# Rounded three-pass downs for seven more units, VectorE making both halves of w1 for the first four experts, in a recurrent layer with a mixture of experts

## The reference, cut to what matters

```python
# x: 32 sequences, 32 steps, 128 features. xw = x @ Wx + b
# scan: h_t = tanh(xw_t + h_(t-1) @ Wh)                      -> 1024 tokens of 128
xn = xf * rsqrt(mean(xf * xf) + EPS) * norm_scale
logits = xn @ wg + bg;  vals, idx = top_k(logits, 4);  gates = softmax(vals)   # spread over 16 experts
h = einsum('th,ehd->etd', xn, w1) + b1                       # 16 experts, 128 -> 256
a = minimum(h[..., ::2], 7.0); b = clip(h[..., 1::2], -7.0, 7.0)
s = a * sigmoid(1.702 * a) * (b + 1.0)
y = einsum('eti,eih->eth', s, w2) + b2                       # 128 -> 128
out = x + xf + einsum('eth,te->th', y, gate_full)
```

## Time and profile before

| | |
|---|---|
| median of 3 runs | 105.08 us (104.44 to 105.55) |
| profiled execution, its time | 105.43 us |
| profiled execution, its span | 103.2 us |
| TensorE busy (matmul) | 97.5 us, 94% |
| VectorE, ScalarE, GpSimd busy | 70.9, 68.8 and 69.2 us |
| one relu, one sigmoid-gelu, one act_high of 512 columns on ScalarE | 0.66, 0.66 and 0.62 us |
| granted TensorE clock | 1.00 |

### The profile page before, as it was taken

How to read it: one execution, slowest core, us unless ns; L and a number is a source line. 1 busy time by engine, 2 the same in 40 slices (tenths; PEclk the granted TensorE clock), 3 DMA queues, 4 the chain that set the end, 5 groups by cost and what they waited for, 6 DMA issues and landing times.

```text
span 103.2 us, 1831 instructions
## 1 busy us (share of the span) xinstructions
PE 97.5 (94%) x587; PEld 82.7 (80%) x588; DVE 70.9 (69%) x181; ACT 68.8 (67%) x162; POOL 69.2 (67%) x82
## 2 busy tenths in 40 slices
PE   7989997999999999999999999999999999999970
PEld 2657556799999799998999788888888888889950
DVE  0300569878859975898669987867886978878530
ACT  3224799799877893669857777556678688697000
POOL 6000287999394998089773999999659459859300
PEclk9999999999999999999999999999999999999999
DMA  2997970005980007960099301996010000000012
GB/s 71 202 295 245 393 291 12 6 10 136 332 341 6 6 6 179 386 248 3 16 267 389 154 0 17 259 352 241 6 51 3 0 0 0 0 0 0 6 51 51
DMA packets 5001, 12.99 MB, mean 126 GB/s; under 512 B 752, under 2 KB 1792, under 8 KB 4992
## 3 DMA queue, kind: packets, MB, share of 16 engines
q1 hardware_dynamic: 4672, 12.66, 36.7%
q10 hardware_dynamic: 320, 0.21, 0.7%
HBM read 12.28 MB, written 0.59 MB: 125 GB/s over the span
## 4 chain that ended last, share of the span: by engine, by line
PE 71%; DVE 13%; DMA 5%; ACT 4%; issue 2%; POOL 1%; SPq 1%; DVEq 0%; POOLq 0%
PE psA L910 19%; PE psB L910 17%; PE psY L954 6%; DMA wx_x_sb<-in_wx_x 5%; PE psR L954 5%; PE psM L945 3%; PE psY L945 3%; DVE lin L788 2%; PE psY L855 2%; DVE act L811 2%; PE psM L966 2%; PE psY L966 2%; PE psM L954 2%; PE psR L855 2%; PE psA L887 1%
## 5 line engine op out<-in xcount | busy, mean ns | idle before, releaser
L788 DVE TENSOR_SCALAR lin<-psB,one_b1b 128x256 f32<-128x256 f32 (+1 forms) x48 | 25.9, 568 | 11.9 <-PE psB L910 11.9
L589 ACT ACTIVATE psA<-psA,lim_b1a 128x256 f32<-128x256 f32 (+1 forms) x48 | 23.8, 511 | 14.1 <-PE psA L910 13.9
L461 POOL TENSOR_TENSOR actg<-act,gate_cols 128x512 f32<-128x512 f32 x25 | 31.8, 1281 | 1.7 <-DMA gate_cols<-gate_rows 1.7
L601 ACT ACTIVATE psA<-psA,limit_col 128x512 f32<-128x512 f32 x32 | 21.1, 658 | 0.8
L910 PE MATMUL psA<-xn_hi,w_hi 128*128 128x256 f32 (+1 forms) x48 | 18.8, 392 | 0.4 <-DVE act L811 0.3
L811 DVE SCALAR_TENSOR_TENSOR act<-lin,psA 128x512 f32<-128x512 f32 x26 | 17.9, 687 | 1.5 <-DVE lin L788 0.9
L910 PE MATMUL psB<-xn_hi,w_hi 128*128 128x256 f32 (+1 forms) x48 | 15.8, 329 | 0.0
L910 PE MATMUL psB<-xn_lo,w_hi 128*128 128x256 f32 (+1 forms) x48 | 15.3, 319 | 0.0
L910 PE MATMUL psB<-xn_hi,w_lo 128*128 128x256 f32 (+1 forms) x48 | 15.3, 318 | 0.0
L910 PE MATMUL psA<-xn_hi,w_lo 128*128 128x256 f32 (+1 forms) x48 | 15.2, 318 | 0.0
L910 PE MATMUL psA<-xn_lo,w_hi 128*128 128x256 f32 (+1 forms) x48 | 15.2, 319 | 0.0
(11 more groups left out here) (113 smaller groups left out, 182.9 us busy)
## 6 DMA issues: line engine op xcount, KB each, us to landing
gate_cols<-gate_rows SPq DMA_DIRECT2D x16, 512.0 KB, 5.4
w_sb<-in_w SPq DMA_DIRECT2D x4, 512.0 KB, 8.4
w_sb<-in_w SPq DMA_DIRECT2D x4, 256.0 KB, 9.6
out<-yT SPq DMA_DIRECT2D x3, 128.0 KB, 1.7
wx_x_sb<-in_wx_x SPq DMA_DIRECT2D x1, 320.0 KB, 5.5
wx_x_sb<-in_wx_x SPq DMA_DIRECT2D x2, 128.0 KB, 2.6
small_h<-in_small ACTq DMA_DIRECT2D x1, 105.0 KB, 2.7
gate_rows<-gT SPq DMA_DIRECT2D x4, 16.0 KB, 1.4
```

Source lines behind the costliest of these rows:

```text
L461: nc.gpsimd.tensor_tensor(by_pair(actg[:, u % SUM_DEPTH, w]), by_pair(act[:, u % ACT_DEPTH, w]), gate_block(u, w), ALU.mult).then_inc(actg ...
L589: last = nc.scalar.activation(psA[u % 2][:, o], psA[u % 2][:, o], ACT.Relu, scale=-1.0, bias=lim_b1a[:, e0 + k:e0 + k + 1])
L601: nc.scalar.activation(psA[u % 2][:, 0:w], psA[u % 2][:, 0:w], ACT.Gelu_apprx_sigmoid, scale=-1.0, bias=limit_col[:, :]).then_inc(swish_do ...
L788: last = nc.vector.tensor_scalar(lin[:, v % 2, o], psB[v % 2][:, o], one_b1b[:, e0 + k:e0 + k + 1], LIMIT + 1.0, ALU.add, ALU.min)
```

## The change

SPLIT grows from 8 units to 15: 12, 13 and 15 (two experts each) and 16 to 27 without a gap. Unit 12 also joins DVE_PRODUCT, so VectorE multiplies it by its gates. All of w2 is now split, in four parts of four experts in place of three runs of 2, 3 and 3. ScalarE makes the high parts at the ends of slots 6, 8, 12 and 14. GpSimd makes the low parts in its slots 9 (two of them), 13 and 16.

VectorE makes both halves of w1 for experts 0 to 3 at the start (w1_halves), where ScalarE made the high halves, and GpSimd and VectorE shared the low halves of experts 0 to 5. VectorE also makes the high half of gS (gates_halves), which was ScalarE's. At the start normalise(1) stands behind route_logits(0). On GpSimd power_rstd of pair 1 moves one slot ahead. On PE one x times Wx product leaves the gap after step 1, which waited for the last part of x, and one goes to the gap after step 7. The result goes to xn in place of yT.

```diff
     GROUP0 = list(range(CHUNKS[0])) + list(range(CHUNKS[0], NT + 1, 2))
-    W1_SHARED = 3
+    W1_DVE = 2
     XW_AT = [0, 3, 0, 1, 2, 1, 2, 3]
-    XW_GAP = {1: 5, 2: 6, 3: 7, 4: 3, 6: 4}
+    XW_GAP = {2: 5, 3: 6, 4: 3, 6: 4, 7: 7}
     NQ = NT // 2
...
     FIRST = UNIT0[NC - 1]
-    SPLIT = [u for u in range(FIRST + 2, NU - 4) if u % 4]
-    SPLIT_RUNS = [[u for u in SPLIT if u // 4 == k] for k in sorted({u // 4 for u in SPLIT})]
-    W2_HIGH, W2_LOW = [13, 14, 17], [16, 17, 18]
+    SPLIT = [FIRST - 4, FIRST - 3, FIRST - 1] + list(range(FIRST, NU - 4))
+    W2_ORDER = [2, 3, 0, 1]
+    W2_HIGH, W2_LOW = [6, 8, 12, 14], [9, 9, 13, 16]
+    EW = E // len(W2_ORDER)
     SPLIT_DEPTH = 3
-    DVE_PRODUCT = list(range(FIRST + 4, NU, 2))
+    DVE_PRODUCT = [FIRST - 4] + list(range(FIRST + 4, NU, 2))
...
     RSTD = [None] + [v + 1 for v in STATS[1:]]
+    POWER = [None, STATS[1] - 1] + STATS[2:]
     GATES = [0] + [v + 2 for v in STATS[1:]]
...
-        def w2_run(i):
-
-            run = SPLIT_RUNS[i]
-            k = SPLIT.index(run[0])
-            return slice(k, k + len(run)), slice(run[0] - FIRST, run[-1] + 1 - FIRST)
+        def w2_part(i):
+
+            return slice(W2_ORDER[i] * EW, (W2_ORDER[i] + 1) * EW)
...
-                pool.wait_ge(w1_hi_ready, 2 * p + a + 1)
+                pool.wait_ge(w1_hi_ready, 2 * (p - W1_DVE) + a + 1)
                 pe_ = slice(2 * p, 2 * p + 2)
...
-                to, es = w2_run(i)
+                es = w2_part(i)
                 pool.wait_ge(w2_hi_ready, i + 1)
-                nc.gpsimd.tensor_tensor(w2_lo[:, to, :], w2_sb[:, es, :], w2_hi[:, to, :].bitcast(F32),
+                nc.gpsimd.tensor_tensor(w2_lo[:, es, :], w2_sb[:, es, :], w2_hi[:, es, :].bitcast(F32),
                                         ALU.subtract).then_inc(w2_lo_ready, 1)
...
             power_rstd(1)
-            for p in range(W1_SHARED):
-                w1_low(p, 1)
+            for a in range(2):
+                w1_low(W1_DVE, a)
             power_expo(0)
             place_expo(0)
-            for p in range(W1_SHARED, NP):
+            for p in range(W1_DVE + 1, NP):
                 for a in range(2):
...
                     xn_low(pair_group(q))
-                for q in at(STATS, v):
+                for q in at(POWER, v):
                     power_rstd(pair_group(q))
+                for i in at(W2_LOW, v):
+                    w2_low(i)
                 for q in at(RSTD, v):
...
                     place_expo(q)
-                for i in at(W2_LOW, v):
-                    w2_low(i)
                 if v >= POOL_LAG and v - POOL_LAG not in DVE_PRODUCT:
...
-            def gates_low(q):
-
-                dve.wait_ge(gS_high, q + 1)
+            def gates_halves(q):
+
+                dve.wait_ge(gT_ready, q + 1)
                 low, qc = slice(LOW_AT, LOW_AT + E), slice(q * PW, (q + 1) * PW)
+                mark(nc.vector.tensor_copy(gS[:, qc], psX[0:GR, 0:PW]))
+                settled()
                 nc.vector.tensor_tensor(gS[low, qc], psX[low, 0:PW], gS[low, qc].bitcast(F32),
...
-            def w1_low(p):
+            def w1_halves(p):
+                dve.wait_ge(w1_loaded[2 * p // EG], 16)
                 pe_ = slice(2 * p, 2 * p + 2)
-                dve.wait_ge(w1_hi_ready, 2 * p + 1)
-                nc.vector.tensor_tensor(w1_lo[:, pe_, 0, :], w1_sb[:, pe_, 0, :], w1_hi[:, pe_, 0, :].bitcast(F32),
+                mark(nc.vector.tensor_copy(w1_hi[:, pe_, :, :], w1_sb[:, pe_, :, :]))
+                settled()
+                nc.vector.tensor_tensor(w1_lo[:, pe_, :, :], w1_sb[:, pe_, :, :], w1_hi[:, pe_, :, :].bitcast(F32),
                                         ALU.subtract).then_inc(w1_ready, 1)
...
             b2_parts()
+            w1_halves(0)
             stats(0)
-            w1_low(0)
+            w1_halves(1)
             normalise(0)
...
             copy_raw(pair_tiles(0), psB[0]).then_inc(raw_read, 1)
-            normalise(1)
             dve.wait_ge(consts_ready, 1)
             dve.wait_ge(bg_loaded, 16)
+            dve.wait_ge(raw_read, 1)
             route_logits(0)
+            normalise(1)
             route_top(0)
...
             route_hot(0)
-            w1_low(1)
-            w1_low(2)
             close_gates(0)
...
                         to = psX[:, 0:w]
+                        dve.wait_ge(gS_ready, NQ if v > LAST_T else NQ - 1)
                     else:
...
                     pe.wait_ge(gS_ready, q)
+                if q == NQ - 1:
+                    pe.wait_ge(actg_dve, 1)
                 for k, j in enumerate(pair_tiles(q)):
...
                     i = SPLIT.index(u)
-                    pe.wait_ge(w2_lo_ready, [u in run for run in SPLIT_RUNS].index(True) + 1)
+                    pe.wait_ge(w2_lo_ready, W2_ORDER.index((e0 + r - 1) // EW) + 1)
                     passes = ((w2_hi, act_hi), (w2_lo, act_hi), (w2_hi, act_lo))
...
                             pe.wait_ge(act_hi_ready, i + 1)
-                        for o, y in y_parts(c):
-                            last = nc.tensor.matmul(y, w[:, i, :], x_part[:, i % SPLIT_DEPTH, o], start=False, stop=False)
+                        for k in range(r):
+                            for o, y in y_parts(c):
+                                a = part(c, k) if r > 1 else o
+                                last = nc.tensor.matmul(y, w[:, e0 + k, :], x_part[:, i % SPLIT_DEPTH, a], start=False,
+                                                        stop=(m == 2 and e0 + k == E - 1))
                     last.then_inc(y_mm, 1)
...
                     x_wx(XW_GAP[t], 1, start=False)
-                elif t == TL + 1:
+                if t == TL + 1:
                     pe.wait_ge(consts_ready, 1)
...
```

More of the change, by code:

```diff
@@ L153, in adaln_rnn_moe_kernel @@
         act_lo = sb("act_lo", [P, SPLIT_DEPTH, W], F32R)
-        w2_hi = sb("w2_hi", [P, len(SPLIT), H], F32R)
-        w2_lo = sb("w2_lo", [P, len(SPLIT), H], F32R)
-        yT = sb("yT", [P, NT * P])
+        w2_hi = sb("w2_hi", [P, E, H], F32R)
+        w2_lo = sb("w2_lo", [P, E, H], F32R)
+        yT = xn
         psA = [pb("psA0"), pb("psA1")]
@@ L198, in adaln_rnn_moe_kernel @@
         gT_ready = sem("gT_ready")
-        gS_high = sem("gS_high")
         gS_ready = sem("gS_ready")
@@ L312, in w1_low_count @@
         def w1_low_count(p, a):
-            return p + 1 if p < W1_SHARED else 2 * p - W1_SHARED + a + 1
+            return p + 1 if p < W1_DVE else 2 * (p - W1_DVE) + a + 1
         def steps_at(u, slot):
@@ L544, in copy_gates @@
                 nc.scalar.activation(gT[:, qc], psX[0:E, 0:PW], ACT.Copy).then_inc(gT_ready, 1)
-                nc.scalar.activation(gS[:, qc], psX[0:GR, 0:PW], ACT.Copy).then_inc(gS_high, 1)
             def act_high(u):
@@ L556, in w2_high @@
             def w2_high(i):
-                to, es = w2_run(i)
+                es = w2_part(i)
                 for g in range(NG):
                     acte.wait_ge(w2_loaded[g], 16)
-                nc.scalar.activation(w2_hi[:, to, :], w2_sb[:, es, :], ACT.Copy).then_inc(w2_hi_ready, 1)
+                nc.scalar.activation(w2_hi[:, es, :], w2_sb[:, es, :], ACT.Copy).then_inc(w2_hi_ready, 1)
             acte.wait_ge(small_loaded, 16)
@@ L570, in _ @@
                 elif t >= W1_AT:
-                    w1_high(t - W1_AT)
+                    w1_high(2 * W1_DVE + t - W1_AT)
             acte.wait_ge(consts_ready, 1)
-            for k in range(HEAD - 1 - W1_AT, 2 * NP):
+            for k in range(2 * W1_DVE + HEAD - 1 - W1_AT, 2 * NP):
                 w1_high(k)
@@ L791, in _ @@
                 for q in at(GATES_T, v - 1):
-                    gates_low(q)
+                    gates_halves(q)
                 if v == LAST_T + 1:
-                    gates_low(NQ - 1)
+                    gates_halves(NQ - 1)
                 for q in at(STATS, v):
@@ L998, in _ @@
                 if c == 0:
-                    pe.wait_ge(w1_ready if v < W1_SHARED else w1_half_ready, w1_low_count(v, 0))
+                    pe.wait_ge(w1_ready if v < W1_DVE else w1_half_ready, w1_low_count(v, 0))
                 if v == UNIT0[c]:
@@ L1011, in _ @@
                     pe.wait_ge(raw_read, 1)
-                if c == 0:
+                if W1_DVE <= v < UNIT0[1]:
                     pe.wait_ge(w1_half_ready, w1_low_count(v, 1))
```

## The result

| | before | after |
|---|---|---|
| first comparison, median (runs) | 105.3 us (104.44 to 105.55, 4) | 106.5 us (105.70 to 106.99, 4) |
| ratio, 95% interval | | 1.0114 [1.0071, 1.0157] |
| second comparison (e8 below), median (runs) | 105.36 us (29) | 106.23 us (105.49 to 106.96, 12) |
| ratio, 95% interval | | 1.0089 [1.0048, 1.0129] |
| profiled execution: time, span | 105.43, 103.2 us | 105.70, 103.9 us |

The changed kernel is about 1% slower. Its page of the profile shows at once that another engine has joined the bound: in the chain of waits TensorE's share falls from 71% to 35%, and GpSimd's rises from 1% to 28%.

A forecast was written before the change was run, and what follows sets the result against it. TensorE was taken as the bound from about 20 us on; -0.98 - 0.05 + 0.30 + 0.50 + 0.40 + 0.73 = +0.90 us on 105.08 gave 106.0 us. Its own range was 105.5 to 106.5 us, with rivals 104.2 to 106.8.

The forecast's parts named there:

- The downs: Seven more units with rounded downs on TensorE, each 0.14 us shorter than plain: -0.98 us, all on the path.
- The start: Pair 0's routing before slot 0: logits held by GpSimd's w1_low, top values as before: -0.05 us, bounds -0.6 and +0.2.
- Slot 2: VectorE's added CAST in gates_halves delays act of unit 2, for which TensorE's slot 4 waits: +0.30 us.
- Slots 9 to 11: Pair 2's logits held by GpSimd's second w2_low, delaying inverse, scaling and TensorE's transposes: +0.50 us, bounds 0 and +0.8.
- Slots 12 to 16: Later act of unit 12 and held pair 3 logits delay act of unit 14: +0.40 us, bounds +0.2 and +0.6.
- The backlog: GpSimd without idle time makes act_lo late for third passes of downs 12 and 13: +0.73 us, bounds 0.4 and 1.1.
- from unit 18 on GpSimd gets ahead: Late in the kernel: act_lo of 15 to 17 covered by the same 0.73 us, then GpSimd ahead; no further cost.
- Rival 1: Logits slip through ahead of GpSimd's operations at the start and slots 9 to 16: 104.8 us, chance 0.25.
- rival 2: Logits unheld and GpSimd's operations in time, only VectorE's two additions remaining: 103.8 us, chance 0.12.
- Rival 3: GpSimd enters slot 14 0.6 us later, delaying units 13 and 17 to the end: 106.6 us or above, chance 0.15.

The follow-up runs named there:

- e8: The changed kernel itself, unchanged, in twelve more executions: 106.23 us, ratio to before 1.0089.
- e2: The changed kernel with the last w2_low on GpSimd in slot 23 in place of slot 16: 106.11 us, ratio to before 1.0061.
- e4: The kernel before with w1_halves, the moved x products and route_logits ahead of normalise(1) alone: 104.91 us, ratio to before 0.9983.
- e1: The changed kernel with the first two w2_low on GpSimd in slots 8 and 11, not both in slot 9: 106.10 us, ratio to before 1.0102.
- e10: The changed kernel with the high half of gS back on ScalarE and four filling matmuls before slot 0: 105.01 us, ratio to before 0.9964.
- e7: The changed kernel with w2_low in slots 8, 11, 13, 23, pair 0's exponentials ahead of two w1_low, and gS's high half on ScalarE: 104.09 us.
- e5: The changed kernel with the downs of units 12, 13 and 15 plain again: 106.12 us, ratio to before 1.0067.
- e11: The changed kernel with the four corrections of e7 and the down of unit 27 plain: 103.91 us, ratio to before 0.9864.

## Why the prediction was right, and where its steps were not

The forecast of 106.0 us for the median was 0.2 to 0.5 us low; the first comparison's 106.5 us is the upper end of its range. As a difference it was +0.90 us, against +1.2 and +0.87 us measured. The sign and the main mechanisms (holds, backlog) were right, but that the sum came so close is partly luck, as the clock, which it doesn't have, makes up for misses of the other sign. By its own steps:

- **The downs, -0.98 us.** Slots 18 and 19 took 4.42 us without waits (e2) against 4.50 before, and the later ones gave 0.88: -0.96 us measured. Right in all; that slots 18 and 19 show so little of it is a matter of where a slot is cut (last section).
- **The start, -0.05 us.** It was -0.42 us, between the bounds. That both logits would be held once each was right, but GpSimd began its w1_low at 13.62 and not at 13.88 us, so that the holds ended earlier, and the first xn_hi came 0.14 us sooner. S holds -0.28 us of it, and e4, the start part by itself, gives -0.32. What I did not see is the price of the new order in the other direction: TensorE idle before slot 0, and with it the clock, some 0.4 us of the median (106.23 against 105.86).
- **Slot 2, +0.30 us.** +0.32 us at slot 4. I said that no gap would take it back; 0.16 us were back by slot 7.
- **Slots 9 to 11, +0.50 us.** +0.45 us; e1 confirms it as the hold. But the w2_low came 0.4 us earlier than I had them (41.56 and not 42.0 us), and it was the first logit and not the second that met the second of them; the size of the hold came out alike. Either edit shortens the same hold: e10 gets 0.30 us of it back without the CAST of slot 8, which I had counted only as 0.45 us on the statistics.
- **Slots 12 to 16, +0.40 us.** +0.32 us, all of it undone in e10, so here it was the CAST, and the hold of pair 3's logits only by way of it. That hold has a narrow margin, though: e7 has it again without the CAST.
- **The backlog, +0.73 us.** 0.85 us in slots 18 and 19 (5.27 against 4.42). Right in place and size.
- **The step that failed** is "from unit 18 on GpSimd gets ahead", and with it that nothing further is to be paid. GpSimd does catch up, once: it waits 0.40 us for act_hi ahead of the act_lo of unit 24. But from there six operations follow without a gap (act_lo of 24, product of 27, act_lo of 25, 26 and 27, product of 29, 89.84 to 97.39 us), where the kernel before had 1.40 us of idle time and five operations. The last downs took 0.31 us longer for it, and the sum had no term for that. e5, in which GpSimd has idle time and the wait stays, and e11, which removed it with one act_lo, show that this end is a cost of its own and not the backlog.

Rival 1 (no hold) and rival 2 (faster) fall with the 1.28 and 1.34 us of the logits. Rival 3 (a longer backlog) is not what happened: the backlog was 0.12 us above its term. The misses partly cancel, -0.37 us at the start and -0.16 us at slot 7 against +0.31 us at the end: -0.42 + 0.32 - 0.16 + 0.45 + 0.32 + 0.85 - 0.96 + 0.31 = +0.71 us in the trace at full clock, and the clock adds 0.4 us to the median, which makes +1.1 us, beside +1.2 and +0.87 us measured. The part of the clock for the whole kernel is a difference of medians of twelve and seven executions, so it is known to some 0.2 us only.

## What to carry to other kernels

A faster instruction on the bounding engine that needs an extra operation of another one is paid from that engine's slack to the very end of the kernel: add up its work per slot against the slot, and look at its last operation, not only at the first that is late, since an engine that has caught up in the middle can still be late with a run of operations at the end. An added VectorE operation has to be followed through everything that is released behind it, GpSimd's order included, and priced again in each slot where it stands. And where work is reordered so that TensorE waits about a microsecond, look at the granted clock of many executions: a single profile can miss the cost.

## What the runs showed of the hardware that I had not expected

- GpSimd gets between two consecutive VectorE operations with two SBUF operands when it has one waiting: at the start both logits were held once each (1.28 us, with 0.38 us unheld). In slot 9 only the first was (1.19 us), by the last GpSimd operation there. Logits that start 0.18 us before the end of the GpSimd operation aren't held (e10).
- An idle microsecond of TensorE was followed by a stretch at half clock in 18 of 69 executions (a mean granted clock of 0.982 to 0.984; the stretch itself was seen in the two that were profiled). It cost 0.64 us in either pair of profiles; 0.9 us of filling matmuls ended that.
- VectorE's CAST of 128x512 from SBUF took 0.43 us, where I had 0.4 to 0.7, about the 0.41 us of the 80x256 from PSUM:

```profile
8.91 0.43 DVE L742 CAST w_hi<-w_sb 128x512 fp32r<-128x512 f32 x1 [4.33 <-DMA w_sb<-in_w]
```

- The saving of a rounded down falls partly into the slot behind it: the first rounded down after a plain one has a slot of 2.29 us and the plain one after it 2.07 us, with 2.24 and 2.10 us inside a series. The two add up to 4.36 us, against 4.34 us in series, so the switch itself shows no price worth counting. That is why slots 18 and 19, with a plain down on either side, gave only 0.08 us.
